# Edge tiles of a graph network: who issues the loads of the sorted rows

## The reference

```python
edge_index = jnp.stack([src, dst])
h = jnp.maximum(_layernorm(x, axis=-1), 0.0)
x = x + _L0_gnn_ref(h, edge_attr_64, ...)       # hidden = leaky_relu([h[dst], edge] @ w1 + b1), summed by src
x = x + _L1_gnn_ref(h, W, attn, rel_emb, src, dst, edge_type_100)   # attention over edges, weight by relation
x = x + _L2_gnn_ref(h, edge_index, W, b)        # h[row] summed by col
x = x + _L3_gnn_ref(h, edge_index, ...)         # x[src] summed by dst
```

## Time and profile before

| | us |
|---|---|
| median of 3 runs | 3945.95 |
| lowest and highest | 3945.78, 3947.28 |
| the profiled execution | 3951.51 |
| its span, first to last instruction | 3949.8 |
| first and last write of the stage issued | 1546.6, 2966.6 |

### The profile page before, as it was taken

The page is one execution under the profiler, slowest core; times in us unless marked ns, Lnnn a source line. Parts: engine busy times, 40 slices in busy tenths (PEclk is TensorE's granted clock), DMA queues, the critical chain, the costliest instruction groups (busy, mean ns, idle before and its releaser), DMA issues. The chain is left out here.

```text
span 3949.8 us, 88026 instructions
## 1 busy us (share of the span) xinstructions
PE 2757.8 (70%) x19674; PEld 2007.0 (51%) x19675; DVE 2593.6 (66%) x7923; ACT 1608.0 (41%) x4084; POOL 2025.6 (51%) x2354
## 2 busy tenths in 40 slices
PE   2314555445455545988888888888898967769599
PEld 2213333333334334888888888888884232234345
DVE  8724555555555555988888888888895669940501
ACT  1001222222222223777777777777774523220201
POOL 0016666666666667888888888888880000000100
PEclk9955666765665577999999999999998979979797
DMA  9972222222222213777777777777774658848082
GB/s 385 414 314 63 65 64 65 62 64 63 66 65 64 65 56 109 208 209 209 210 209 209 209 209 209 209 208 210 208 212 178 249 216 293 290 158 316 8 332 99
DMA packets 702423, 696.70 MB, mean 176 GB/s; under 512 B 51182, under 2 KB 633536, under 8 KB 692640
## 3 DMA queue, kind: packets, MB, share of 16 engines
q1 hardware_dynamic: 672386, 636.28, 51.6%
q0 software_dynamic: 25792, 54.52, 4.1%
q10 hardware_dynamic: 4190, 5.22, 0.4%
HBM read 340.91 MB, written 354.90 MB: 176 GB/s over the span
## 5 line engine op out<-in xcount | busy, mean ns | idle before, releaser
L893 POOL DMA_INDIRECT sorted_rows<-rows,posi x806 | 782.5, 971 | 556.2 <-issue 324.2
L1173 DVE SCALAR_TENSOR_TENSOR acc<-acc,keep,pm 128x256 f32<-128x256 f32 x1504 | 717.8, 477 | 155.2 <-DMA count_matrices<-acc 96.0
L841 PE MATMUL s_peq<-sb_w1bb,eT 128*128 128x256 f32 x806 | 388.1, 582 | 560.2 <-ACT eT L708 456.0
L1004 POOL TENSOR_SCALAR ohs_e<-iota,rt 128x128 f32<-128x128 f32 x1128 | 672.7, 611 | 11.4 <-DMA rt<-sorted_rows 11.4
L1100 PE MATMUL pm<-ohw_e,ohs_e 128*128 128x128 f32 x3008 | 662.7, 302 | 0.0
L1013 POOL TENSOR_TENSOR hid<-pre_e,excess 128x512 f32<-128x512 f32 x376 | 533.5, 1419 | 223.0 <-ACT excess L1040 223.0
L1106 PE MATMUL px<-PN,dT 128*128 x4512 | 498.6, 219 | 0.2 <-ACT dT L1047 0.2
L841 PEld LDWEIGHTS s_peq<-sb_w1bb,eT 128*128 128x128 f32 x806 | 188.3, 286 | 606.7 <-ACT eT L708 476.9
L1056 ACT ACTIVATE ohw_e<-ohd_e,rt 128x128 f32<-128x128 bf16 x1504 | 474.6, 386 | 0.0
L1100 PEld LDWEIGHTS pm<-ohw_e,ohs_e 128*128 128x128 f32 x3008 | 459.7, 193 | 0.0
L1099 PE MATMUL pm<-ohd_e,ohs_e 128*128 128x128 bf16 x1504 | 334.3, 222 | 153.6 <-DVE acc L1173 137.3
(11 more groups left out here) (299 smaller groups left out, 4479.3 us busy)
## 6 DMA issues: line engine op xcount, KB each, us to landing
count_matrices<-acc SPq DMA_DIRECT2D x1504, 128.0 KB, 2.1
ab<-count_matrices SPq DMA_DIRECT2D x75, 1600.0 KB, 7.9
sorted_rows<-zrow SPq DMA_DIRECT2D x188, 528.0 KB, 10.4
rt<-sorted_rows SPq DMA_DIRECT2D x376, 264.0 KB, 3.1
arb<-count_matrices SPq DMA_DIRECT2D x25, 1664.0 KB, 6.8
arb<-count_matrices SPq DMA_DIRECT2D x25, 1536.0 KB, 6.5
ef<-in_edge_attr_dram SPq DMA_DIRECT2D x58, 364.0 KB
sorted_rows<-rows,posi POOLq DMA_INDIRECT x806
```

Of the source, the lines that this page charges most:

```text
L841: nc.tensor.matmul(pe_q[:, q % 2, 0:2 * D], eT[:, q % 2, :], w1bb[:], start=True, stop=True).then_inc(s_q, 1)
L893: pool.indirect_dma_start(sortd, bass.IndirectOffsetOnAxis(ap=posi[:, h, c:c + 1], axis=0), rows[:, h, c, :], None).then_inc(s_sc[h], 16)
L1004: last = nc.gpsimd.tensor_scalar(ohs[:, k % BUFS, j, :], iota128[:], rt[:, k, j, D + 1:D + 2], None, ALU.is_equal)
L1173: nc.vector.scalar_tensor_tensor(acc[:, k % SUMS, j, :], before, keep[:, at:at + 1] if isinstance(at, int) else keep[:, ds(at, 1)], pm[:, ...
```

## The change

The rows are loaded two groups at a time: one transfer of 128 x 8 rows in place of two of 128 x 4. Four semaphores in `s_rt` take the place of eight, and all who wait for rows wait for the pair's. Of `rt` nothing changes. The first four transfers (all eight places) still go out from SyncE. All others go out from ScalarE: at the end of its step n, if n is even, it waits until groups n - 2 and n - 1 are done with their rows and loads the pair that comes four pairs after them, groups n + 6 and n + 7. SyncE keeps only the writes, all 47 passes of them in one loop. ScalarE's last pass now stands outside its loop, because only its step 0 has a load.

```diff
@@ load, and SyncE
-            sv = sortd.rearrange("(n j p) w -> n p j w", p=P, j=G)
+            sv = sortd.rearrange("(m j p) w -> m p j w", p=P, j=2 * G)
...
+            def load(eng, m, r):
+                eng.dma_start(rt[:, 2 * r:2 * r + 2, :, :].rearrange("p k j w -> p (k j) w"),
+                              sv[ds(m, 1)].squeeze(0)).then_inc(s_rt[r], 16)
+
+            def load_freed(eng, i, k, final):
+                if k % 2 == 0 and not (final and k):
+                    n = i * RING + k
+                    eng.wait_ge(s_pre, n)
+                    eng.wait_ge(s_ow, n)
+                    eng.wait_ge(s_os, n)
+                    eng.wait_ge(s_o3, n)
+                    if k:
+                        load(eng, (i + 1) * (RING // 2) + k // 2 - 1, k // 2 - 1)
+                    else:
+                        load(eng, i * (RING // 2) + RING // 2 - 1, RING // 2 - 1)
...
-                        if more and j == 2:
-                            sp.wait_ge(s_pre, n + 2)
-                            sp.wait_ge(s_ow, n + 2)
-                            sp.wait_ge(s_os, n + 2)
-                            sp.wait_ge(s_o3, n + 2)
-                            load(n + 1 + RING, (k + 1) % RING)
                         sp.wait_ge(s_acc, n * G + j + 1)
...
-                for r in range(RING):
-                    load(r, r)
...
+                for r in range(RING // 2):
+                    load(sp, r, r)
+                with sp.Fori(0, LOOPS) as i:
                     for k in range(RING):
-                        step(i, k, True)
...
@@ GpSimd and VectorE, three places
-                    pool.wait_ge(s_rt[k], i * 16 + 16)
+                    pool.wait_ge(s_rt[k // 2], i * 16 + 16)
...
@@ ScalarE
                     last.then_inc(s_ow, 1)
+                    if not (first and k == 0):
+                        load_freed(act, i, k, final)
```

More of the change, by code:

```diff
@@ L927, in build @@
             s_k = sem("e_constants")
-            s_rt = [sem("e_rows%d" % r) for r in range(RING)]
+            s_rt = [sem("e_rows%d" % r) for r in range(RING // 2)]
             s_od = sem("e_dst_onehots")
@@ L946, in build, with step @@
             block = ctx.enter_context(nc.Block())
-            sv = sortd.rearrange("(n j p) w -> n p j w", p=P, j=G)
+            sv = sortd.rearrange("(m j p) w -> m p j w", p=P, j=2 * G)
             GROUPS = LOOPS * RING
+            def load(eng, m, r):
[12 more added lines that the diff above has]
+                        load(eng, i * (RING // 2) + RING // 2 - 1, RING // 2 - 1)
             @block.sync
             def _(sp):
-                def load(n, r):
-                    sp.dma_start(rt[:, r, :, :], sv[ds(n, 1)].squeeze(0)).then_inc(s_rt[r], 16)
-                def step(i, k, more):
+                def step(i, k):
                     n = i * RING + k
@@ L975, in step @@
                                      acc[:, k % SUMS, j, :].rearrange("p (a c) -> p a c", a=2)).then_inc(s_w[k % SUMS], 16)
-                for r in range(RING):
-                    load(r, r)
[L979 to L984, removed]
-                    for k in range(RING):
-                        step(i, k, True)
[L987 to L990, removed]
+                for r in range(RING // 2):
+                    load(sp, r, r)
+                with sp.Fori(0, LOOPS) as i:
+                    for k in range(RING):
+                        step(i, k)
                 for p in range(SUMS):
@@ L1040, in negative, with step @@
                     nc.scalar.activation(excess[:, k % 2, :, :], pre[:, k % 2, :, :], ACT.Relu, scale=-0.8).then_inc(s_y, 1)
-                def step(i, k, first):
+                def step(i, k, first, final):
                     n = i * RING + k
@@ L1057, in step @@
                     last.then_inc(s_ow, 1)
+                    if not (first and k == 0):
+                        load_freed(act, i, k, final)
                 for k in range(RING):
-                    step(0, k, True)
-                with act.Fori(1, LOOPS) as i:
+                    step(0, k, True, False)
+                with act.Fori(1, LOOPS - 1) as i:
                     for k in range(RING):
-                        step(i, k, False)
+                        step(i, k, False, False)
+                for k in range(RING):
+                    step(LOOPS - 1, k, False, True)
                 negative(LOOPS - 1, RING - 1, False)
@@ L1149, in onehots @@
                     n = i * RING + k
-                    dve.wait_ge(s_rt[k], i * 16 + 16)
+                    dve.wait_ge(s_rt[k // 2], i * 16 + 16)
                     if not (first and k < BUFS):
```

## The result

| | before | after |
|---|---|---|
| median of 4 runs each, us | 3945.86 | 3839.62 |
| lowest and highest | 3942.04, 3947.28 | 3835.83, 3846.8 |
| span of the profiled execution | 3949.8 | 3834.1 |
| us per group, groups 8 to 368 | 3.788 | 3.504 |

What follows compares the result with a forecast made beforehand. SyncE's sequencer was taken as the bound at 3.788 us per group; the DVE and PE loop of 3.47 plus 0.24 / 2 gives 3.59, so 360 groups save 71 us: 3875 us, range 3830 to 3920.

Steps and rivals of the forecast that it cites:

- SyncE's sequencer was the bound: Edge tiles: SyncE's queue of loads and writes, period 3.73 us, sets the 3.79 us per group.
- part 1: SyncE's queue: the load and its waits cost 0.77 us per group; without them its period falls from 3.73 to 2.96.
- The next bound, the loop of 3.47 us over DVE and PE: Edge tiles: `pre_e`, third and fourth additions, PE's last two tiles: 0.73 + 1.00 + 0.53 + 1.21 = 3.47 us per group.
- One in two is long: DVE's register load before the third addition: every second one meets arriving rows, adding 0.24 / 2 to 3.47, giving 3.59 us.
- two kinds of read: DVE's register load (L62): about 0.55 us when it meets arriving rows, 0.31 when not, a difference of 0.24.
- rival (a): DVE's register load escapes the arriving rows: 3.47 us per group, 114 us gained, 3832 us; chance 0.18.
- ScalarE pays nothing: ScalarE's load issue is covered by 2.2 us of queued activations: cost 0, upper end 0.05 us per group, 18 us.
- Small terms: Edge tiles: first rows up to 0.8 us later, taken as 0; no wait from the shorter lead; last groups unchanged.
- (b): Every DVE register load is long: 3.71 us per group, 28 us gained, 3918 us; chance 0.20.
- (c): The DMA engines, with 2.96 us of work per group, become the bound and nothing moves: 3946 us; chance 0.05.
- (d): ScalarE's load issue stalls, at 4.40 us each: 4.69 us per group, 4270 us; chance 0.05.
- (e): ScalarE's load waits for something slower: rows come later but in time, and the gain stays; no chance given.

Runs made afterwards that it cites:

- e10: Kernel before with double loads issued by SyncE and DVE's register load moved behind the dispatch of the destination onehots: 3.461 us per group, ratio to before 0.9701.
- e8: Changed kernel with a second DVE register load between `pre_e` and the third addition: 3.861 us per group, ratio to the kernel before 1.0088.
- e5: Changed kernel with ScalarE's load waiting for the `ohw_e` of its own group: 3.479 us per group, ratio to the kernel before 0.9699.
- e9: Changed kernel with DVE's register load moved behind the dispatch of the destination onehots, before the fourth addition: 3.373 us per group, ratio to the kernel before 0.9597.
- e1: Changed kernel with ScalarE loading one group in every step instead of pairs: 3.491 us per group, ratio to the kernel before 0.9721.

## Why the prediction was right, and which term was off

- **SyncE's sequencer was the bound: right, shown.** One DMA issue and four waits less, and DVE's wait for writes is gone; register loads added to SyncE alone bring it back, with the period close to the sum of SyncE's parts in three kernels (4.30 against 4.285, 4.12 against 4.107, 3.47 against 3.461). These sums rest on the 2.96 and 0.77 us of part 1, for which e10's queue has 2.93 and 0.79, and on reads as each run measured them.
- **The next bound, the loop of 3.47 us over DVE and PE: right, shown** by e8 (+0.357 for one more read in it) and e9 (-0.121 for the read taken out). With every read at its floor (e5) the loop took 3.479 us.
- **"One in two is long": the term that was mis-sized.** The forecast put 0.24 / 2 = 0.12 us on top of 3.47. It measured 0.031: the read's mean is 0.338, of which 0.307 is the floor. Every second read does fall among arriving rows, as the prediction timed it, but only a third of these is long. That term is 0.089 us x 360 = 32 of the 35 us between forecast and result. The prediction's two kinds of read exist, and their distance was nearly right (0.53 and 0.31 in the kernel before); the mistake was to put the long ones down to arriving rows, beside which e9's reads stay short. In the kernel before they were those close behind SyncE's writes, which the change moved as well; that is a pattern, not a shown cause. With all its weight on that one cause, the prediction gave rival (a), where the read escapes, only 0.18; the result, 3.504, lies 0.034 above (a)'s 3.47, nearer to it than to 3.59. That the time is inside the range is the work of its lower bound, (a).
- **ScalarE pays nothing: right; its upper end of 18 us was too high.** The issue began 0.58 behind `excess` (0.65 forecast) and took 0.44 us. Without cover (e5) the cost is still none.
- **Small terms: right.** The first addition of the stage came at 1544.8 (before 1545.9), no engine waited for `rt` from 1574 to 2830 us, and the double load landed in 4.3 us where 4.5 was taken.
- **Rivals.** (b) fell with the register load. (c) fell: the DMA share is 0.81, and e9 ran at 0.86. (d) fell: no issue of the load took more than 0.46 us between the posts. What held the 4.40 us issue of the earlier trace rows no run shows. (e) fell.
- **The rule of the Trainium skill** ("DMA: Bandwidth & Descriptors", sections "Rules for kernel authors" and "Issuing engines are not separate DMA queues"): what another issuer saves is issue time, and the trace and e1 agree. The issue is small beside the transfer here too, 0.39 us of the 3.1 to the landing, so the trace doesn't contradict the second section as the prediction has it. What counts is its share of the issuing queue: with its waits 0.77 of 3.79 us of SyncE's period, and 0.28 us of each group's time once it was gone.

## What to carry over

When no engine and no DMA share is full and yet an engine waits for a transfer that lands quickly, lay the issue of the transfer beside the end of the work it belongs to: nine microseconds between the two, with no wait of its own in front, was here a sequencer that is full, although the issues themselves are only half of its period (4 x 0.37 and 0.39 of 3.79 us). Add up such a queue by its rows (issue, register loads, waits, branch), take from it what another queue can issue under its own work, and then ask for the next loop in the same terms, since here a register load in DVE's queue without a long operation ahead of it was paid in full (e8) and behind one of 0.68 us it was free (e9). And when a duration's median lies far above its floor, sort its instances by what stands near them before making one cause of it: here the reads went with the neighbour that was not suspected, and the change moved both.

## What was not expected of the hardware

- A register load of two values took 466 ns or more, 653 in the median of 584; of one value on SyncE 273, of four 301 to 366, by kernel.
- The same register load took 305 to 310 ns or about 500, in DVE's queue and in SyncE's, and in most runs, not in all, the long ones stood 0.6 to 1.1 us behind the issue of a write by SyncE. The cause is open.
- A wait of 0.8 us put into ScalarE's queue in every second group cost nothing, although its idle time per group is 0.67 us.
